# Decoder layer on one core: fp16 pairs for cross attention's projections, whole-batch 1/std on GpSimd, and new instruction lists

## The reference

```python
x = x + attn(layernorm(x))          # stream A: q, k, v with 128 features, softmax(q k^T / sqrt(128)) v, then w_o
x = x + xattn(layernorm(x), ctx)    # stream B (and E for the context's side)
x = x + ffn(layernorm(x))           # stream C: ternary weights, 8-bit activations, silu(gate) * up, down

def xattn(x, y, mask, W, b):
    x_proj = relu(x @ W.T + b)      # 512x256
    y_proj = relu(y @ W.T + b)
    scores = x_proj @ y_proj.T      # 512x512, masked columns -inf
    return softmax(scores) @ y
```

## Time and profile before

| engine | busy us | share of the span | instructions |
|---|---|---|---|
| TensorE, matmuls (PE) | 332.2 | 95% | 1813 |
| TensorE, weight loads (PEld) | 220.3 | 63% | 1838 |
| VectorE (DVE) | 298.6 | 85% | 862 |
| ScalarE (ACT) | 285.2 | 82% | 532 |
| GpSimd (POOL) | 296.0 | 85% | 503 |

### The profile page before, as it was taken

How to read it: one execution, slowest core, us unless ns; L and a number is a source line. 1 busy time by engine, 2 the same in 40 slices (tenths; PEclk the granted TensorE clock), 3 DMA queues, 4 the chain that set the end, 5 groups by cost and what they waited for, 6 DMA issues and landing times.

```text
span 349.3 us, 6994 instructions
## 1 busy us (share of the span) xinstructions
PE 332.2 (95%) x1813; PEld 220.3 (63%) x1838; DVE 298.6 (85%) x862; ACT 285.2 (82%) x532; POOL 296.0 (85%) x503
## 2 busy tenths in 40 slices
...
PEclk9999978999999999999999999999999999999999
...
GB/s 262 423 262 85 122 134 266 90 176 53 109 156 93 176 129 241 136 143 211 168 185 205 94 223 197 155 132 164 239 79 115 117 135 126 47 89 199 62 120 123
DMA packets 132264, 54.49 MB, mean 156 GB/s; under 512 B 124672, under 2 KB 126336, under 8 KB 131840
## 3 DMA queue, kind: packets, MB, share of 16 engines
...
...
## 4 chain that ended last, share of the span: by engine, by line
PE 48%; POOL 15%; ACT 10%; DVE 10%; issue 9%; DMA 5%; SPq 2%; ACTq 0%; DVEq 0%; POOLq 0%
PE b_bank L1204 6%; PE b_bank L1206 6%; PE b_bank L1205 6%; PE d_bank L1437 4%; PE g_bank L1417 4%; PE u_bank L1417 4%; PE a_bank L1204 3%; PE a_bank L1206 3%; PE a_bank L1205 3%; POOL b_p L710 2%; PE a_bank L1288 2%; POOL p L706 2%; POOL c L745 2%; DMA b_p16T<-b_p 2%; ACT a_p L989 2%
## 5 line engine op out<-in xcount | busy, mean ns | idle before, releaser
L1091 ACT ACTIVATE c_work<-g_bank,c_tanh_scale 128x512 f32<-128x512 f32 x52 | 35.4, 681 | 16.2 <-PE g_bank L1417 14.6
L710 POOL TENSOR_TENSOR b_p<-b_p 128x512 f16<-128x512 f32 x32 | 37.1, 1165 | 3.4 <-ACT b_p L1000 2.9
L1684 DVE TENSOR_TENSOR c_work<-c_work,u_bank 128x512 f32<-128x512 f32 x52 | 35.3, 679 | 2.6 <-PE u_bank L1417 2.2
L1204 PE MATMUL b_bank<-c,b_p16T 128*128 128x256 f16 x128 | 34.9, 273 | 1.5 <-DMA b_p16T<-b_p 1.5
L1689 DVE SCALAR_TENSOR_TENSOR c_work<-c_work,g_bank 128x512 f32<-128x512 f32 x50 | 33.8, 676 | 2.8 <-ACT c_work L1091 2.6
L706 POOL TENSOR_TENSOR p<-a_p,p 128x512 f16<-128x512 f32 x28 | 32.4, 1168 | 3.6 <-ACT p L945 3.6
L1206 PE MATMUL b_bank<-c,b_p16T 128*128 128x256 f16 x128 | 34.9, 273 | 0.0
L1205 PE MATMUL b_bank<-c,b_p16T 128*128 128x256 f16 x128 | 34.9, 273 | 0.0
L1417 PE MATMUL u_bank<-upT,xqT 128*128 128x512 bf16 x102 | 31.3, 380 | 1.5 <-DVE c_work L1684 0.7
L1417 PE MATMUL g_bank<-gateT,xqT 128*128 128x512 bf16 x99 | 30.6, 380 | 1.9 <-ACT xqT L1068 1.0
L1437 PE MATMUL d_bank<-downT,c_half 128*128 128x256 bf16 x240 | 31.2, 273 | 1.0 <-DVE x_all L1694 0.5
...
## 6 DMA issues: line engine op xcount, KB each, us to landing
...
```

Of the source, the lines that this page charges most:

```text
L710: pool.tensor_tensor(b_p16[:, t, S:2 * S], b_p[:, t, :], b_p16[:, t, 0:S], ALU.subtract).then_inc(b_p_los, 1)
L1091: act.activation(gate_tile(j, n), gu_bank("g", j, n), ACT.Silu if (n, j) in SILU else ACT.Tanh, scale=c_tanh_scale[:, j // 2:j // 2 + 1]). ...
L1204: pe.matmul(dst, l_hi, r_hi, start=first, stop=False)
L1684: dve.tensor_tensor(h_tile(j // 2, n)[:, (j % 2) * HALF:(j % 2 + 1) * HALF], gate_tile(j, n), gu_bank("u", j, n), ALU.mult).then_inc(hs, 1)
```

## The change

Cross attention's two projections are written as fp16 pairs in place of fp32r pairs, with a factor `PROJ_SCALE` = 2^-15 in the activation so that they fit. The scale of batch 0's context, which the kernel before worked out but did not use for the projection, is now part of it (`y_scale`), so batch 0's projection waits for its own power step; its squares are taken from `b_xn` in place of `ctx_raw`. The sum of squares of W also takes in the bias. Stream A's 1/std of batches 2 to 7 and stream B's of batches 3 to 7 are made for four columns at once (`a_rstd_whole`, `b_rstd_whole`); the latter makes the negated 1/std first, and then all four shifts in one instruction. All five lists are ordered anew.

```diff
+PROJ_SCALE = 2.0 ** -15
+B_APART = 3
-A_FRONT = "... P1/0 SS/1 Q/1 ... YP1/1 SS/0 Y1/0"
+A_FRONT = "... P1/0 SS/0 Q/1 ... YP1/1 SS/1 Y1/0"
 PE_ORDER
...
-    E.YP1/1 A.S2/1 A.Y1/0 A.S3/1 A.Q/2 A.K/2 E.SS/2 B.XT0/0 B.XT1/0 B.XP0/0 B.XP1/0 A.H/1 B.S0/0 A.Y0/1 B.S1/0
-    A.Y1/1 B.S2/0 B.S3/0 E.YP0/2 A.V/2 A.S0/2 B.O0/0 A.S1/2 A.S2/2 A.S3/2 B.O1/0 B.O2/0 B.O3/0 B.XT0/1 B.XT1/1
+    A.S2/1 F.total/0 A.Y1/0 A.S3/1 A.Q/2 A.K/2 E.SS/2 B.XT0/0 B.XT1/0 A.H/1 B.XP0/0 B.XP1/0 A.Y0/1 A.Y1/1 B.S0/0
+    B.S1/0 B.S2/0 B.S3/0 E.YP0/2 A.V/2 A.S0/2 B.O0/0 A.S1/2 A.S2/2 B.O1/0 A.S3/2 B.O2/0 B.O3/0 B.XT0/1 B.XT1/1
...
 ACT_ORDER
-    W.sq/0 W.qkv/0 A.xT0/1 A.Q/0 A.xT1/1 W.r/0 E.sq/1 W.hi/0 A.VT/0 A.exp0/0 A.exp1/0 W.va/0 E.hi/1 E.YP0/0 A.exp2/0
+    A.xT0/1 W.qkv/0 A.xT1/1 A.Q/0 W.sq/0 W.r/0 E.sq/0 E.sq/1 A.VT/0 A.exp0/0 A.exp1/0 A.P0/0 W.hi/0 W.va/0 A.exp2/0
...
-    E.hi/0 A.exp0/1 A.P0/1 E.YP1/1 A.exp1/1 A.P1/1 B.norm0/0 A.exp2/1 A.exp3/1 A.P2/1 A.P3/1 A.K/2 E.sq/2 B.norm1/0
-    B.XT0/0 B.XT1/0 B.mask/0 E.hi/2 B.XP0/0 B.XP1/0 A.H/1 A.Q/2 F.sign0/0 F.sign1/0 B.exp0/0 B.P0/0 B.exp1/0 B.P1/0
+    E.hi/0 A.exp0/1 A.P0/1 E.YP1/1 A.exp1/1 A.P1/1 A.exp2/1 A.P2/1 A.exp3/1 A.P3/1 E.sq/2 A.K/2 B.norm0/0 B.norm1/0
+    A.Q/2 B.XT0/0 E.hi/2 B.XT1/0 F.sign0/0 A.H/1 B.XP0/0 B.XP1/0 F.sign1/0 B.mask/0 B.exp0/0 B.P0/0 B.exp1/0 B.P1/0
...
 POOL_ORDER
-    E.sc/0 E.YP0/1 E.lo/0 B.rs0/0 A.P0/1 A.P1/1 B.rs1/0 A.P2/1 A.P3/1 E.pow/2 E.sc/2 F.round0/0 E.lo/2 B.XP0/0
+    E.sc/0 E.YP0/1 E.lo/0 A.P0/1 B.rs0/0 A.P1/1 A.P2/1 A.P3/1 B.rs1/0 E.pow/2 E.sc/2 F.round0/0 E.lo/2 E.YP1/1
...
-        yp_hi, yp_lo = (sb(f"yp_{s}", [P, YP_SLOTS, DC, S], F32R) for s in ("hi", "lo"))
-        xp_hi, xp_lo = (sb(f"xp_{s}", [P, DC, S], F32R) for s in ("hi", "lo"))
+        yp_hi, yp_lo = (sb(f"yp_{s}", [P, YP_SLOTS, DC, S], F16) for s in ("hi", "lo"))
+        xp_hi, xp_lo = (sb(f"xp_{s}", [P, DC, S], F16) for s in ("hi", "lo"))
...
             def c_powers_of(n):
-                if n > 0:
-                    pool.wait_ge(c_powers, c_rank(n))
-                    pool.wait_ge(W_scaled, 2)
...
+                pool.wait_ge(c_powers, n + 1)
+                pool.wait_ge(W_scaled, 2)
+                if n == 0:
+                    pool.tensor_scalar(y_scale[:, :], c_pow[:, 0, 0:1], w_pow[:, 0:1], PROJ_SCALE, ALU.mult, ALU.mult)
...
...
-            def a_rstd_part(half, n):
+            def a_rstd_whole(n):
+                pool.wait_ge(a_mvs, 2 * n + 2)
+                pool.wait_ge(a_rstds, 4 * n)
+                if n > 2:
+                    pool.wait_ge(r_stored, 16 * (n - 2))
+                pool.wait_ge(a_maxed, T * (n - 1))
+                pool.tensor_tensor(a_var[:, :], a_mv[:, :, 1], eps[:, :], ALU.add).then_inc(a_rstds, 2)
+                pool.wait_ge(a_rstds, 4 * n + 2)
+                pool.tensor_tensor(a_rstd[:, n % 2, :], a_var[:, :], neg_half[:, :], ALU.pow).then_inc(a_rstds, 2)
+
+            def b_rstd_whole(n):
+                pool.wait_ge(b_mvs, 2 * n + 2)
+                pool.wait_ge(b_xns, 2 * n)
+                pool.tensor_scalar(b_var[:, :], b_mv[:, :, 1], EPS, X_SCALE ** -2, ALU.add, ALU.mult).then_inc(b_rstds, 2)
+                pool.wait_ge(b_rstds, 4 * n + 2)
+                pool.tensor_tensor(b_rstd[:, :], b_var[:, :], neg_half[:, :], ALU.pow).then_inc(b_rstds, 2)
+                pool.wait_ge(b_rstds, 4 * n + 4)
+                pool.tensor_scalar(b_neg[:, :], b_rstd[:, :], -1.0, 1.0, ALU.mult, ALU.mult).then_inc(b_negs, 1)
+                pool.wait_ge(b_negs, n - B_APART + 1)
+                pool.tensor_tensor(b_shift[:, :], b_mv[:, :, 0], b_neg[:, :], ALU.mult).then_inc(b_shifts, 2)
...
             def yp_relu(c, n):
-                b = bias[:, c:c + 1] if n == 0 else y_bias[:, n, c:c + 1]
-                act.activation(e_relu[:, :], a_bank(f"YP{c}", n)[:, :], ACT.Relu, bias=b)
-                act.activation(yp_hi[...], a_bank(f"YP{c}", n)[:, :], ACT.Relu, bias=b).then_inc(e_relus, 1)
+                scale = y_scale[:, :] if n == 0 else PROJ_SCALE
+                b = y_bias[:, n, c:c + 1]
+                act.activation(e_relu[:, :], a_bank(f"YP{c}", n)[:, :], ACT.Relu, scale=scale, bias=b)
+                act.activation(yp_hi[...], a_bank(f"YP{c}", n)[:, :], ACT.Relu, scale=scale, bias=b).then_inc(e_relus, 1)
...
             def square_W():
-                act.activation(w16[...], W_raw, ACT.Square, accum_out=w_ss[:, :]).then_inc(W_squared, 1)
+                act.wait_ge(small_loaded, 16)
+                act.activation(w16[...], W_raw, ACT.Square, accum_out=w_ss[:, 0:1])
+                act.activation(w_bias[:, :], bias, ACT.Square, accum_out=w_ss[:, 1:2]).then_inc(W_squared, 1)
...
             def square_ctx(n):
-                act.wait_ge(ctx_loaded, 16 * c_rank(n))
+                if n == 0:
+                    act.wait_ge(ctxT0_loaded, 16)
+                else:
+                    act.wait_ge(ctx_loaded, 16 * c_rank(n))
```

More of the change, by code:

```diff
@@ L118 @@
[L118 to L137, removed]
@@ new lines @@
+    C.g2/0 A.K/3 C.u2/0 A.V/3 C.g3/0 B.O0/1 A.S0/3 C.g4/0 A.S1/3 B.O1/1 C.u3/0 C.g5/0 B.O2/1 B.O3/1 C.u4/0 A.S2/3
+    B.XT0/2 B.XT1/2 A.S3/3 C.g6/0 E.YP0/3 C.u5/0 B.XP0/2 B.XP1/2 C.DN0/0 E.YP1/3 C.u6/0 C.g7/0 B.S0/2 C.u7/0 C.DN1/0
+    C.g0/1 B.S1/2 B.S2/2 C.g1/1 C.u0/1 B.S3/2 E.SS/4 C.u1/1 A.H/3 C.g2/1 C.DN2/0 A.Y0/3 C.u2/1 C.DN3/0 C.g3/1 A.Y1/3
+    C.u3/1 B.O0/2 C.g4/1 B.O1/2 C.u4/1 A.Q/4 C.g5/1 B.O2/2 C.u5/1 A.K/4 B.O3/2 A.V/4 B.XT0/3 C.g6/1 B.XT1/3 E.YP0/4
+    C.u6/1 C.DN0/1 C.g7/1 A.S0/4 B.XP0/3 C.u7/1 B.XP1/3 E.YP1/4 C.DN1/1 A.S1/4 A.S2/4 C.g0/2 B.S0/3 A.S3/4 C.g1/2
@@ new lines @@
+    C.u0/2 C.DN2/1 B.S1/3 C.g2/2 B.S2/3 C.u1/2 B.S3/3 C.u2/2 C.g3/2 C.DN3/1 E.SS/5 A.H/4 C.u3/2 B.O0/3 A.Y0/4 A.Y1/4
+    C.g4/2 C.u4/2 B.O1/3 C.g5/2 A.Q/5 A.K/5 C.g6/2 B.O2/3 C.u5/2 B.O3/3 B.XT0/4 C.u6/2 C.g7/2 B.XT1/4 C.DN0/2
+    E.YP0/5 B.XP0/4 B.XP1/4 C.u7/2 A.V/5 C.DN1/2 B.S0/4 B.S1/4 C.g0/3 A.S0/5 B.S2/4 C.u0/3 A.S1/5 C.g1/3 A.S2/5
+    C.u1/3 C.DN2/2 A.S3/5 C.g2/3 C.DN3/2 C.u2/3 B.S3/4 C.g3/3 B.O0/4 C.u3/3 E.YP1/5 C.g4/3 C.u4/3 B.O1/4 C.g5/3
+    E.SS/6 A.H/5 C.g6/3 C.u5/3 C.DN0/3 A.Y0/5 A.Y1/5 B.O2/4 C.g7/3 A.Q/6 A.K/6 B.O3/4 A.V/6 A.S0/6 C.g0/4 B.XT0/5
@@ new lines @@
+    B.XT1/5 C.u6/3 C.DN1/3 A.S1/6 C.u7/3 A.S2/6 B.XP0/5 B.XP1/5 C.u0/4 C.g1/4 A.S3/6 E.YP0/6 C.DN2/3 B.S0/5 B.S1/5
+    C.u1/4 C.DN3/3 C.g2/4 B.S2/5 C.u2/4 C.g3/4 B.S3/5 C.u3/4 A.H/6 E.YP1/6 A.Y0/6 A.Y1/6 C.g4/4 E.SS/7 A.Q/7 B.O0/5
+    A.K/7 C.g5/4 B.O1/5 C.u4/4 C.g6/4 B.O2/5 B.O3/5 C.g7/4 B.XT0/6 B.XT1/6 C.u5/4 A.V/7 A.S0/7 B.XP0/6 B.XP1/6
+    A.S1/7 A.S2/7 C.DN0/4 C.u6/4 C.g0/5 A.S3/7 B.S0/6 C.u7/4 B.S1/6 C.g1/5 B.S2/6 E.YP0/7 C.g2/5 C.u0/5 B.S3/6
+    C.u1/5 C.g3/5 A.H/7 C.u2/5 C.DN1/4 C.u3/5 A.Y0/7 A.Y1/7 C.g4/5 C.u4/5 B.O0/6 C.DN2/4 B.O1/6 B.O2/6 C.g5/5 B.O3/6
```

304 lines of the change are left out of this document (156 added, 148 removed).

## The result

The changed kernel took 354.55 us (median of 20 runs, 349.59 to 356.01), the kernel before 350.42 us (20 runs, 348.96 to 352.89). The ratio is **1.0074 [1.005, 1.0099]**: slower by 2.6 us, where I had forecast 5.4 us less.

What follows compares the result with a forecast made beforehand. The prediction took TensorE's summed matmuls to bound three quarters of the run, with engine chains in 40 to 57 us and at the end; -2.9 - 1.0 - 1.5 = -5.4 us from 350.1 gave 344.7 us, range 339.0 to 350.5.

Steps and rivals of the forecast that it cites:

- Part 1: Scores' matmuls on TensorE in fp16: 192 matmuls start 0.015 us closer, counted in full, -2.9 us (ends 0 and -6.1).
- Part 2 and 3: GpSimd's fp16 low parts and four-column 1/std: 12.9 us less busy, worth -1.0 us through TensorE's waits in 57 to 320 us.
- Part 3: 1/std for four columns: -1.0 us (ends 0, -4); its 1.45 us more latency per batch before XT0 costed at 0.
- the third rival: Whole-batch 1/std holds up XT0 in batches 3 to 7: 5 x 1.45 = 7.3 us, total 353.5; chance 0.15.
- turning point of 5.4: Whole-batch 1/std latency before XT0 makes the change slower once more than 5.4 of its 7.3 us is uncovered.
- Part 4: New lists in 40 to 57 us: earlier squares, H/1 before XP0, Y steps before S0/0; -1.5 us (ends -7.7, +2.6).
- Part 5: Front (0 to 40 us) and tail reordered: front 0 (ends -1, +1.5), tail 0 (ends -2, +2).
- (a): 40 to 57 us: ScalarE and GpSimd steps reordered, so squares and P transposes come some 1 us earlier; about half of -1.5.
- (c): Before S0/0: both Y steps of batch 1 stand after XP1 and cover the relus and low parts of XP.
- a sign of being wrong: TensorE's granted clock falling at a second place, besides the fall expected near 50 us, would show the forecast wrong.

Runs made afterwards that it cites:

- fp16_alone: The kernel before with only the projections' pairs in fp16 (batch 0's with a constant factor), old lists and halves of 1/std: 350.04 us, ratio 0.9967.
- old_to_33: The changed kernel with the old order of every list, loads included, up to about 33 us and batch 0's constant factor: 350.16 us, ratio 0.9994.
- old_to_57: The changed kernel with the old order of every list up to about 57 us and batch 0's constant factor: 350.16 us, ratio 0.9966.
- after_qkv_first: The changed kernel with its first two loads exchanged back, w_qkv first as in the kernel before: 351.2 us, ratio 1.002.
- old_to_95_again: Repeat run of the changed kernel with the old order of every list up to about 95 us and batch 0's constant factor: 350.04 us, ratio 0.9981.
- new_lists_whole_fp32r: The changed kernel with the two projections' pairs back in fp32r, new lists and whole 1/std kept: ratio 1.0165 to the kernel before.

## Why the prediction was wrong, by its own steps

**Part 1** (-2.9). The term was right for what TensorE's work loses, and the rows' 0.015 us stands (0.217 for 0.23): in the new lists fp16 brings 2.9 us with whole 1/std, 2.1 with halves. Both contain GpSimd's shorter low parts as well, which no run keeps apart. In the old lists only 1.2 arrive, and there I had mis-sized the term: I counted it in full. I had both ends (0 and -6.1) and named the reason for the one at 0.

**Part 2 and 3, GpSimd's work** (-12.9 us busy): 283.2 for 296.0, -12.8. I had made it worth -1.0 in time. In the new lists whole 1/std as it stands, latency and all, is worth -2.5 against halves, but the new lists are slow with halves (1.0152). Against fp16_alone (0.9967) whole 1/std with the new order behind 95 us brings nothing that these runs can tell (0.9952, 0.9981).

**Part 3, the latency costed at 0.** Right for the new lists, wrong as a statement on the change alone: in the old ones it costs 6.4 us, at the place and nearly at the price of the third rival. So this is not where the changed kernel lost. My reason for the 0 was weak, though. I had counted ten or more entries between Y1 and XT0; in batches 3 to 7 there are 12, 10, 8, 12 and 8, in the old list 12, 12, 7, 6 and 5, and the longest wait with old lists came in batch 4, behind twelve. There ScalarE makes two other copies (0.67 and 0.58 us) between the two pairs of norm copies; in the new list all four stand together. Which of the two hides it is not tested. (The rival's 353.5 also leaves out Part 4's -1.5, which its turning point of 5.4 counts; with it, it is 352.0.)

**Part 5, the front costed at 0** (ends -1, +1.5): **this is the first failed step.** It costs 2.9 us. I had counted ScalarE's squares and passed over the first line of SP's list, where w_qkv moved from first to second. TensorE's first real work hangs on that load; it was right behind the warm-up (3.94) and now waits 1.13 us. Of the 2.9 us, 1.6 to 2.1 are this load's, by the two exchanges; the rest appears at the wait for context 1's transposes, and its cause is not tested. I had read "38.2 of 40 us busy, with matmuls that nothing shortens" as cover. A stretch in which TensorE is full is not covered against a late start: with the load second, Q/2 came 2.0 us later and the kernel took 2.1 us more.

**Part 4, 40 to 57 us costed at -1.5: the second failed step.** Measured between old_to_33 and old_to_57 the new order of this stretch costs 0.3% (1.0 us), uncertain by about as much; a gain of 0.43% is outside that. Their timelines, old_to_33 (new order here) first, both with Y0 and Y1 ahead of S0/0:

```profile
43.79 0.38 PE L1341 MATMUL e_bank<-c_ss,ones 128*128 128x1 f32 x2 [1.18 <-ACT c L1073]
45.35 0.53 PE L1356 MATMUL b_bank<-ident,b_xn 128*128 128x128 f32 x2 [1.17 <-ACT b_xn L946]
46.86 1.54 PE L1356 MATMUL b_bank<-ident,b_xn 128*128 128x128 f32 x6 [0.98 <-ACT b_xn L946]
...
58.27 0.39 PE L1231 MATMUL b_bank<-yp_hi,xp_hi 128*128 128x512 f16 x1 [0.86 <-POOL xp_lo L760]
```

```profile
44.85 0.39 PE L1341 MATMUL e_bank<-c_ss,ones 128*128 128x1 f32 x2 [2.35 <-ACT c L1073]
...
58.38 0.38 PE L1231 MATMUL b_bank<-yp_hi,xp_hi 128*128 128x512 f16 x1
```

(a) The squares do come 1.1 us earlier in the new order, as I had worked out. But I had counted norm0 of batch 0, moved behind the P steps, as 1.1 us of ScalarE saved and not as a wait: XT0/0 and XT1/0 now wait 1.17 and 0.98 us for `b_xn`, and in the end S0/0 starts 0.1 us earlier, not 1.5. (b) In the changed kernel not even the squares are early (45.12, before 45.14): TensorE arrives 1.2 us later there, and the whole stretch is late with the front. (c) The Y steps ahead of S0/0 cover XP's low parts except 0.86 us, but stand for 1.9 us in front of it. (d) H/1 ran at half clock from 49.01 (0.50 in 50 to 52 us), as the XP step had before. That the clock was 0.90 for 0.80 is not shown to be the order's doing: old_to_33 and after_qkv_first, with TensorE's order as in the changed kernel from 33 us on, have 0.80. I had also read the earlier trace rows too loosely: before, the clock came back at 54.4 us, in H/1 and not in XP, and the matmuls ahead of S0/0 took 8.0 us for 5.2, so 2.8 of the 3.4 us of lost clock fell on matmuls.

**The middle.** I expected 4 us or less of idle in 57 to 320 us; it was 7.5. The extra lies in 57 to 100 us:

```profile
57.00:100.00 43.00, 38.54 (x201) 22.86 (x200) 31.86 (x110) 39.05 (x75) 38.04 (x61) 1.00 0.59 124
```

That is 4.5 us of idle, where the kernel before has 1.6. Two waits of its timeline lead:

```profile
70.57 0.50 PE L1233 MATMUL a_bank<-k_hi,q_hi 128*128 128x512 f32 x1 [1.79 <-DVE vT L1629]
...
83.76 0.38 PE L1233 MATMUL a_bank<-p16T,v16T 128*128 128x512 f16 x1 [1.33 <-DMA p16T<-p]
```

Before, the first of them was 0.49 us. But this idle time is not what made the kernel slower: the cut kernels idle 4.6 us (old_to_33), 2.9 (old_to_57) and 1.7 (old_to_95_again) in the same stretch, and their times lie within 0.3% of each other (0.9994, 0.9966, and 0.9967 on the mean of two runs). Most of what TensorE idles here comes back further on. In the typical execution the first of the two waits is 1.98 us, and TensorE's clock falls a second time behind it, which I had named as a sign of being wrong:

```profile
72.00:78.00 6.00, 6.00 (x30) 4.31 (x31) 4.31 (x16) 5.05 (x12) 4.69 (x8) 0.72 0.64 117
```

The same stretch in the fastest execution has a clock of 1.00. At 0.72 over 6 us that is 1.7 us, and with the 1.7 of the front it makes 3.4 of the 4.5 us between the two profiles. This is a description of two executions, not a tested cause: old_to_57, after_qkv_first and old_to_33 have the same wait (2.0, 2.0 and 1.7 us) in their profiles without the fall, and new_lists_whole_fp32r has the fall (0.72 in 72 to 78 us).

**The two rules that I weighed.** By the Trainium skill, "TensorE: Matmul & The Clock Gate", section "Back-to-back issue gap", the gap of a pair of matmuls taken by itself depends on columns alone, and by that Part 1 would bring 0; the section also says that in a stream the weight loads count. Neighbouring starts went from 0.23 to 0.217 us, and fp32r against fp16 in the same lists gave 2.1 to 2.9 us, so the rows were right. The section "HAM oscillation — how this bites in real kernels", that matmuls behind a wait run cold, fits H/1 and the stretch at 72 us, though not each such wait brought a fall. It does not fit the weight sums: they took 0.68 us behind a wait of 0.70, and 1.19 us before, behind no wait at all.

**The chain of kernels beside the sum.** Each step is a difference of two ratios to before. fp16 alone: -1.2 us, I had -2.9. Whole 1/std with the new order behind 95 us: +6.4 and -6.4, together 0, I had -1.0. The new order in 57 to 95 us: 0. In 33 to 57 us: +1.0, I had -1.5. The front: +2.9, I had 0. The four misses (1.7, 1.0, 2.5 and 2.9) are the 8 us between -5.4 and +2.6. Each step is uncertain by 1.2 to 1.6 us, so only the front's and the two of 6.4 us stand clear by themselves.

**The chances.** The sum was the fault, not the spread: my four terms were nearly independent in my working, and the table above shows that they are not. I gave 0.14 to slower, all of it to the whole 1/std. No rival named the front or the lists themselves as the cost, although the diff rewrote all five lists and I had traced them closely only in 40 to 57 us.
